# Channel statistics as raw moments of even and odd pixels, summed on TensorE in place of being aggregated on VectorE

## The reference, cut to what matters

```python
def group_norm(x, groups):
    xr = x.reshape(B, groups, -1)
    return ((xr - xr.mean(-1)) * rsqrt(xr.var(-1) + 1e-5)).reshape(x.shape)
x = group_norm(hidden_state, 32)                  # gn1: groups of 2 channels
x = silu(conv2d(x, w0, b0))
x = group_norm(x, 16)                             # gn2: groups of 4 channels
x = silu(conv2d(x, w1, b1, padding=1, groups=4))
x = group_norm(x, 2)                              # gn3, with window gating behind it (gna)
...                                               # gating, 1x1 product with `weight`
x = group_norm(v, 32) + hidden_state              # gn4: groups of 2 channels
...                                               # causal attention over the images, then the experts
```

## Time and profile before

| | before |
|---|---|
| median of 3 runs | 162.06 us (161.11 to 162.81) |
| the profiled execution | 162.24 us |
| its span, first to last instruction | 160.4 us |
| mean granted TensorE clock | 0.989 |
| DVE busy | 100.5 us (63%), 384 instructions |
| ACT busy | 77.0 us (48%), 131 instructions |
| POOL busy | 31.0 us (19%), 27 instructions |
| DMA | 4.63 MB, most of it before 10 us |

### The profile page before, as it was taken

The page is one execution under the profiler, slowest core; times in us unless marked ns, Lnnn a source line. Parts: engine busy times, 40 slices in busy tenths (PEclk is TensorE's granted clock), DMA queues, the critical chain, the costliest instruction groups (busy, mean ns, idle before and its releaser), DMA issues.

```text
span 160.4 us, 2711 instructions
## 1 busy us (share of the span) xinstructions
PE 138.7 (86%) x1001; PEld 62.1 (39%) x1001; DVE 100.5 (63%) x384; ACT 77.0 (48%) x131; POOL 31.0 (19%) x27
## 2 busy tenths in 40 slices
PE   4299689999499769797996989998899999999991
PEld 1144244464134227454824613465244524322230
DVE  0775686695876775618997571078634497993631
ACT  0005400320780042780612999964898869709600
POOL 7046100202130025604046070000610000000000
PEclk9999999999959999999999999999999999999999
DMA  4980000000000000000000000000000000001132
GB/s 119 413 319 1 0 2 4 0 4 0 0 6 0 0 0 0 0 4 0 2 0 0 2 4 0 0 0 0 4 0 0 0 4 0 0 18 48 39 96 65
DMA packets 3740, 4.63 MB, mean 29 GB/s; under 512 B 208, under 2 KB 3408, under 8 KB 3600
## 3 DMA queue, kind: packets, MB, share of 16 engines
q1 hardware_dynamic: 3584, 4.27, 7.7%
q10 hardware_dynamic: 144, 0.20, 0.6%
HBM read 3.42 MB, written 1.05 MB: 28 GB/s over the span
## 4 chain that ended last, share of the span: by engine, by line
PE 61%; DVE 19%; ACT 10%; issue 3%; DMA 2%; POOL 2%; DVEq 0%; ACTq 0%
PE bank L805 10%; PE bank L954 9%; PE bank L929 8%; PE bank L942 7%; PE bank L770 4%; PE bank L763 3%; DMA xin<-x 2%; PE bank L822 2%; PE bank L847 2%; ACT h L400 2%; PE bank L855 2%; DVE ctxs L671 2%; PE bank L750 2%; ACT x L358 2%; PE bank L841 2%
## 5 line engine op out<-in xcount | busy, mean ns | idle before, releaser
L400 ACT ACTIVATE h<-bank,s_bnb,s_bns 128x512 f32<-128x512 f32 x32 | 23.2, 779 | 7.5 <-PE bank L929 7.4
L770 PE MATMUL bank<-warm 128*128 128x512 bf16 x80 | 21.0, 401 | 1.1 <-ACT y L337 1.1
L929 PE MATMUL bank<-xs,par 64*64 64x512 f32 x128 | 17.3, 611 | 1.4 <-ACT h L400 1.4
L805 PE MATMUL bank<-pad,w 32*64 32x512 f32 x288 | 17.0, 593 | 0.4 <-DVE pad L504 0.4
L942 PE MATMUL bank<-h,f2s 64*64 64x512 f32 x128 | 17.0, 602 | 0.2
L337 ACT ACTIVATE y<-bank,par 128x512 f32<-128x512 f32 x8 | 4.8, 688 | 21.0 <-PE bank L805 21.0
L763 PE MATMUL bank<-warm 128*128 128x512 bf16 x32 | 10.9, 487 | 1.3 <-POOL warm L304 1.3
L770 PEld LDWEIGHTS bank<-warm 128*128 128x128 bf16 x80 | 7.8, 106 | 9.9 <-issue 3.1
L805 PEld LDWEIGHTS bank<-pad,w 32*64 32x64 f32 x288 | 7.3, 130 | 7.4 <-issue 5.9
L547 DVE BATCH_NORM_STATS2 s_ws<-y 128x6 f32<-128x64 f32 x64 | 8.8, 209 | 0.3 <-ACT y L337 0.2
L329 ACT ACT_TABLE_LOAD x1 | 1.3, 1283 | 13.9 <-PE bank L776 13.9
(11 more groups left out here) (253 smaller groups left out, 251.3 us busy)
## 6 DMA issues: line engine op xcount, KB each, us to landing
par<-params SPq DMA_DIRECT2D x1, 1516.0 KB, 8.8
xin<-x SPq DMA_DIRECT2D x4, 256.0 KB, 4.3
out<-act SPq DMA_DIRECT2D x4, 256.0 KB, 2.2
row_par<-row_params SPq DMA_DIRECT2D x2, 160.0 KB, 8.7
w<-conv_w SPq DMA_DIRECT2D x1, 288.0 KB, 5.0
par<-params ACTq DMA_DIRECT2D x1, 193.5 KB, 3.8
```

The costliest lines, as they stand in the source:

```text
L400: A.activation(h1[(2 * m + h) % 4][:], bank[Z1[h]][:], ACT.Relu, bias=tile("bnb", P, 3 * EP)[:, col:col + 1], scale=tile("bns", P, 3 * EP) ...
L770: T.matmul(bank[Z1[0]][:], warm[:, 0:P], warm[:], start=True, stop=True)
L805: ins = T.matmul(bank[CONV1[k][2 * j + h]][at:at + C, :], w1[rows, tap, :], pad[rows, b:b + 2, dy:dy + S, dx:dx + S], start=(tap == 0), st ...
L929: ins = T.matmul(bank[Z1[h]][to, :], f1[own, e, to], xs[own, k, q], start=True, stop=True)
```

## The change

After `bn_stats`, DVE no longer aggregates. It squares the eight means (even and odd, four pairs) and scales them by 128, the number of pixels in a half, in one instruction (L481 of the changed kernel), and raises a new semaphore, `moments_ready`, with the last `bn_stats`. PE multiplies the group's matrix with the raw numbers: once with mean and sum of squared deviations of the even pixels (8 columns), once with those of the odd ones, added in PSUM; after `stats_ready` it adds the two sets of squares (4 columns each) onto the second half of the columns. The matrices are divided by the number of pixels, and `group_finish` and `group_shift` multiply the mean by 128 again (`unit`).

```diff
+HALF_PIX = PIX // 2
...
-            def group_finish(name, n, rows=P):
+            def group_finish(name, n, rows=P, unit=1.0):
                 t, _, _ = var_tiles[name]
                 ms, sq = tile(t + "ms", rows, 2, n), tile(t + "sq", rows, n)
                 dve.wait_ge(small_ready, SMALL_AT[name])
                 V.tensor_copy(ms, bank[SMALL][0:rows, 0:2 * n].rearrange("p (a n) -> p a n", a=2)).then_inc(small_free, 1)
                 dve.wait_ge(small_free, SMALL_AT[name])
-                step(V.tensor_tensor(sq, ms[:, 0, :], ms[:, 0, :], ALU.mult))
+                step(V.scalar_tensor_tensor(sq, ms[:, 0, :], unit * unit, ms[:, 0, :], ALU.mult, ALU.mult))
                 V.scalar_tensor_tensor(tile(t, rows, n), ms[:, 1, :], EPS, sq, ALU.add, ALU.subtract).then_inc(var_ready, 1)
-            def group_shift(name, n, rows=P, signal=None):
+            def group_shift(name, n, rows=P, signal=None, unit=1.0):
                 t, _, _ = var_tiles[name]
                 dve.wait_ge(rstd_ready, VAR_AT[name])
-                ins = V.scalar_tensor_tensor(tile(t + "nb", rows, n), tile(t + "ms", rows, 2, n)[:, 0, :], -1.0, rstd(name),
-                                             ALU.mult, ALU.mult)
+                ins = V.scalar_tensor_tensor(tile(t + "nb", rows, n), tile(t + "ms", rows, 2, n)[:, 0, :], -unit, rstd(name), ALU.mult, ALU.mult)
                 if signal is None:
                     step(ins)
                 else:
...
             def channel_stats(name, source, n, arrived=None):
                 t, _, _ = var_tiles[name]
-                raw, mv, e2 = tile(t + "raw", P, n, 6), tile(t + "mv", P, n, 2), tile(t + "e2", P, 2, n)
+                raw, sq = tile(t + "raw", P, n, 6), tile(t + "rsq", P, n, 2)
                 for i in range(n):
                     if arrived is not None:
                         arrived(i)
                     ins = V.bn_stats(raw[:, i, :], source(i))
-                step(ins)
-                for i in range(n):
-                    ins = V.bn_aggr(mv[:, i, :], raw[:, i, :])
-                step(ins)
-                V.tensor_copy(e2[:, 0, :], mv[:, :, 0])
-                step(V.tensor_tensor(e2[:, 1, :], mv[:, :, 0], mv[:, :, 0], ALU.mult))
-                V.tensor_tensor(e2[:, 1, :], e2[:, 1, :], mv[:, :, 1], ALU.add).then_inc(stats_ready, 1)
+                ins.then_inc(moments_ready, 1)
+                dve.wait_ge(moments_ready, MOMENTS_AT[name])
+                means = raw.rearrange("p n (a t) -> p n a t", a=2)[:, :, :, 1]
+                V.scalar_tensor_tensor(sq, means, float(HALF_PIX), means, ALU.mult, ALU.mult).then_inc(stats_ready, 1)
...
+            def moments_product(name, matrix):
+                n = PK
+                t = var_tiles[name][0]
+                raw = tile(t + "raw", P, n, 6).rearrange("p n (a t) -> p a t n", a=2)
+                sq = tile(t + "rsq", P, n, 2).rearrange("p n a -> p a n")
+                small(name)
+                pe.wait_ge(moments_ready, MOMENTS_AT[name])
+                for a in range(2):
+                    T.matmul(bank[SMALL][:, 0:2 * n].rearrange("p (t n) -> p t n", t=2), matrix, raw[:, a, 1:3, :], start=(a == 0), stop=False)
+                pe.wait_ge(stats_ready, STATS_AT[name])
+                for a in range(2):
+                    ins = T.matmul(bank[SMALL][:, n:2 * n], matrix, sq[:, a, :], start=False, stop=(a == 1))
+                ins.then_inc(small_ready, 1)
...
-                "warm": warm_up, "heat": keep_warm, "gn1": lambda k: group_product(("gn1", k), w("gn1"), tile(f"gn1v{k}e2", P, 2 * PK), P, 2 * PK),
-                "xnorm": conv0, "gn2": lambda k: group_product(("gn2", k), w("gn2"), tile(f"gn2v{k}e2", P, 2 * PK), P, 2 * PK),
+                "warm": warm_up, "heat": keep_warm, "gn1": lambda k: moments_product(("gn1", k), w("gn1")),
+                "xnorm": conv0, "gn2": lambda k: moments_product(("gn2", k), w("gn2")),
-                "outp": out_product, "gn4": lambda k: group_product(("gn4", k), w("gn1"), tile(f"gn4v{k}e2", P, 2 * PK), P, 2 * PK),
+                "outp": out_product, "gn4": lambda k: moments_product(("gn4", k), w("gn1")),
...
-    put("gn1", (rows[:, None] // 2 == rows[None, :] // 2) / f(2))
-    put("gn2", (rows[:, None] // 4 == rows[None, :] // 4) / f(4))
+    put("gn1", (rows[:, None] // 2 == rows[None, :] // 2) / f(2 * PIX))
+    put("gn2", (rows[:, None] // 4 == rows[None, :] // 4) / f(4 * PIX))
```

More of the change, by code:

```diff
@@ L187, in conv_attention_experts @@
         stats_ready = sem("stats_ready")
+        moments_ready = sem("moments_ready")
         pads_zeroed, consts_ready, warm_ready = sem_list("pads_zeroed", "consts_ready", "warm_ready")
@@ L234, in conv_attention_experts @@
         SMALL_AT = positions({"gn1", "gn2", "s2row", "gn3", "w2", "gna", "w3", "gn4", "score", "logits", "wt", "wb"})
+        MOMENTS_AT = positions({"gn1", "gn2", "gn4"})
         STATS_AT = positions({"gn1", "gn2", "gn3", "w2", "gna", "w3", "gn4"})
@@ L489, in normalise_x @@
             def normalise_x(k):
-                r, nb = group_shift(("gn1", k), PK)
+                r, nb = group_shift(("gn1", k), PK, unit=HALF_PIX)
                 for i in range(PK):
@@ L499, in normalise_0 @@
             def normalise_0(k):
-                r, nb = group_shift(("gn2", k), PK)
+                r, nb = group_shift(("gn2", k), PK, unit=HALF_PIX)
                 dve.wait_ge(pads_zeroed, k + 1)
@@ L615, in residual1 @@
             def residual1(k):
-                group_shift(("gn4", k), PK, signal=gn4_shift_ready)
+                group_shift(("gn4", k), PK, signal=gn4_shift_ready, unit=HALF_PIX)
                 for i in range(PK):
@@ L720, in _ @@
             stages = {
-                "gn1": gn1_stats, "gn1f": lambda k: group_finish(("gn1", k), PK), "xnorm": normalise_x,
-                "gn2": gn2_stats, "gn2f": lambda k: group_finish(("gn2", k), PK), "norm0": normalise_0,
+                "gn1": gn1_stats, "gn1f": lambda k: group_finish(("gn1", k), PK, unit=HALF_PIX), "xnorm": normalise_x,
+                "gn2": gn2_stats, "gn2f": lambda k: group_finish(("gn2", k), PK, unit=HALF_PIX), "norm0": normalise_0,
                 "bn": lambda k: batch_norm_variances(), "bnf": lambda k: fold_weights(),
@@ L726, in _ @@
                 "w2": window_half, "gna": window_norm_stats, "gnaf": lambda k: group_finish(("gna", k), BK, C),
-                "wan": window_normalise, "gate": gate_y, "gn4": gn4_stats, "gn4f": lambda k: group_finish(("gn4", k), PK),
+                "wan": window_normalise, "gate": gate_y, "gn4": gn4_stats, "gn4f": lambda k: group_finish(("gn4", k), PK, unit=HALF_PIX),
                 "x1": residual1, "ln1": lambda n: layer_norm_stats("ln1", n), "hn": lambda k: layer_norm_scale("ln1", k, hn_ready),
```

## The result

The changed kernel takes 164.12 us (median of 4 runs, 162.50 to 164.84) against 162.38 for the kernel before on the same chip: a ratio of 1.0125, 95% interval 1.0078 to 1.0171. Six more runs of the same kernel beside other runs of before gave 1.0124 (1.0069 to 1.0179). All ratios are taken over the runs within 1.5% of the fastest of their kernel. The change makes the kernel slower by about 2 us. The profiled execution took 164.33 us with a span of 162.5, 2.09 us more than that of before.

The account below looks back on a forecast made before the run. No engine was taken to bound the kernel throughout; up to conv0 PE's queue decides, elsewhere DVE's latency where PE waits. Terms 0.37 + 1.26 - 0.22 + 0.66 - 0.20 - 0.22 = +1.65 us gave 163.7, range 162.6 to 165.0.

Parts of the forecast that it names:

- Eight records for each product, the load of each as its price, whatever the columns: All six products: 2 records become 8; six more cost 1.26 us in the first stage, 0.66 later.
- the 0.66 forecast: At ("gn2", 1), inside PE's conv1 stream: six more records cost +0.66 us and delay the whole of conv1.
- The start 0.88 us earlier where PE waits, -0.20 to -0.22 a place: ("gn2", 0), ("gn4", 0), ("gn4", 1): product starts 0.86 to 0.88 us earlier, records cost 0.66; net -0.22, -0.20, -0.22.
- ("gn1", 0) +0.37, ("gn1", 1) +1.26: First stage: an earlier start of 0.89 us against 1.26 for records at the first product; no gain and +1.26 at the second.
- The first stage is the whole loss, the rest cancels: Three small gains, -0.22, -0.20 and -0.22, pay for +0.66 at ("gn2", 1); the first stage's +0.37 and +1.26 are left.
- Both ways to conv0 lead back to the end of the second product, and neither has slack: Before conv0: DVE's copy and `xnorm`, and PE's warm-up matmuls, both follow the second gn1 product and end nearly together.
- The clock in conv0: conv0's first records: clock level least known; unchanged pace keeps the sum, a clock risen by 13.7 us gives back 0.74.
- The rival that the clock comes at the same time as before: At conv0: clock rises at its old time, so +1.65 - 0.74 = +0.91, 163.0 us; chance 0.2.
- the forecast's own allowance of +0.25: At conv0: +0.25 us on the sum if not even its second record gets a share of the faster clock.
- The stretch at the lower clock behind the windows: Between 44 and 46 us: rival that a 2 us shift spares it, -0.7, giving 163.0, or lengthens it; chance 0.08.
- the forecast's half-chances on either side of 1%: Whole kernel: forecast on the edge of 160.4 to 163.7, its chance halved; slower 0.43, same 0.52, faster 0.05.

Follow-up runs that it names:

- the pair taken out: Changed kernel without one pair of warm-up matmuls between the second gn1 product and conv0: ratio 1.0053, on a repeat 1.008; median of the first eight runs 163.74 us.
- the mixed one: Against the kernel before: two-matmul form at (gn1, 0), (gn2, 0), (gn4, 0), (gn4, 1), DVE aggregation at (gn1, 1), (gn2, 1); ratio 0.9853, 159.2 us.
- the two-matmul form everywhere: Raw moments in two matmuls of 16 and 8 columns instead of the changed kernel's four, at all six products; ratio to the kernel before 0.988, 159.5 us.
- the one with gn1 as before: Changed kernel with gn1 aggregated on DVE as before, gn2 and gn4 in the four-matmul form; ratio to the kernel before 1.001.
- a third with the same queue up to there: Four-matmul form only at (gn2, 0), (gn4, 0) and (gn4, 1), the other three aggregated on DVE; ratio to the kernel before 0.9975.

## Why the prediction was right

It forecast 163.7 us, 162.6 to 165.0, and the mechanism, the place and the size of the loss were those of the runs. That the forecast came so near to 164.12 is in part luck: the sum takes the clock of one execution of before, in which it rose in conv0; of two others with the same queue ahead of conv0 one did the same (1.60 us for its first matmul), and the other had it earlier (1.14); and the median of before moved by 0.32 us, from 162.06 to 162.38, with one more run. Point by point:

- *Eight records for each product, the load of each as its price, whatever the columns.* Right. Six more records took 1.29 us at the lower clock with nothing else changed, where 1.26 was forecast, and the loads of the kernel before follow the columns of weights. At ("gn2", 1) conv1 moved from +1.56 to +2.22, the 0.66 forecast. Sixteen columns in a record cost no more than eight.
- *The start 0.88 us earlier where PE waits, -0.20 to -0.22 a place.* Right. The three copies moved by -0.21 (from +1.77, where `bn_stats` stood, to +1.56), -0.21 and, by ACT's copy behind it, -0.21. Squares caused no second wait.
- *("gn1", 0) +0.37, ("gn1", 1) +1.26.* Right: +0.32 (of it -0.06 by the images) and +1.26, and conv0 at 13.69 where 13.72 stood.
- *The first stage is the whole loss, the rest cancels.* Right within the intervals: 1.0117 with gn1 alone, 1.001 (0.9973 to 1.0047) with all but gn1.
- *"Both ways to conv0 lead back to the end of the second product, and neither has slack".* Right for the changed kernel, by the pair taken out. Incomplete for the kernel before: a third way, over POOL, ended 0.11 us ahead of them. It mattered to no term of the sum.
- *The clock in conv0.* The rival that the clock comes at the same time as before is out, in both profiles: conv0's first matmul took 1.74 and 1.86 us, not 0.86 plus its latency. From conv0's start to the end of ACT's wait the first profile lost 0.16 us of the forecast's own allowance of +0.25; in the second, from conv0 to `bn_stats`, it is 0.29 (3.94 us in place of 3.65), a little over it. Executions of the changed kernel with an early clock are not excluded by this, since only two were profiled.
- *The stretch at the lower clock behind the windows.* It was neither spared nor the same. It came with the shift of the stage, and the windows of the changed kernel (us; busy and records of PE, PEld, DVE, ACT, POOL; granted clock, DMA) answer to the earlier trace rows:

```profile
44.00:46.00 2.00, 0.38 (x4) 0.42 (x6) 1.96 (x15) 2.00 (x5) 0.00 (x0) 1.00 0.00 0
46.00:48.00 2.00, 1.98 (x5) 0.54 (x4) 1.90 (x15) 2.00 (x5) 0.00 (x0) 0.52 0.00 0
48.00:50.00 2.00, 2.00 (x8) 0.92 (x8) 1.38 (x12) 1.77 (x4) 0.66 (x1) 0.62 0.00 0
```

It took 0.27 us more before the ("gna", 0) product than in the kernel before (+2.23 to +2.50). This and the 0.16 in conv0 are what the sum lacked: +1.65 forecast, 1.65 + 0.27 + 0.16 = 2.08, 2.09 measured between the two profiled executions. Both are the clock, both differ from one execution to the next (the profiles of five of the kernels above, the mixed one among them, have no such stretch there, and two of the five have one later, the two-matmul form everywhere at 72 to 76 us with a granted clock of 0.50 and 0.75), and so the forecast's half-chances on either side of 1% were about as good as could be said. The result fell on the slower side.

## What to carry to other kernels

Moving small arithmetic from an engine with latency to PE is priced in records, each an f32 load of 128 columns of weights, 0.11 us at the higher clock and 0.21 at the lower, and not in the columns of the product; so put operands side by side in one matmul and let the instruction that empties PSUM do the addition. Do it where PE sits idle waiting for the result, and leave the longer way on the other engine where PE comes late anyway: the same edit was worth -0.2 us at three places, +0.7 at a fourth and +1.3 at a fifth. Idle waiting alone is no warrant: at ("gn1", 0) PE waits too (4.02 us in the kernel before), but it stands at the lower clock there, and the edit cost 0.3 to 0.4. Ask of every place first which engine is late there, and then at which clock PE works there.

## What the runs showed of the hardware

- The moment at which TensorE's clock rises in the first stage, read from the pace of its records, differs between executions of the same queue. Conv0's first matmul took 1.57 and 1.60 us in the kernel before and in the one with gn1 as before, and 1.14 in a third with the same queue up to there; it took 1.74 and 1.86 in two executions of the changed kernel. The second gn1 product, eight records behind one and the same queue, took 0.65 + 0.85 us in both of those and 0.65 + 0.49 and 0.39 + 0.46 in two executions of the kernel without the pair behind it: there the clock rose at about 11 us, and in the changed kernel at about 15.3 and 16.3. Whether thin records delay the rise isn't shown; these last two have the same thin records.
- A kernel with fewer warm-up matmuls ahead of conv0 had times in two groups, 162.4 to 162.7 and 164.1 to 165.7.
- Taking 0.85 us of warm-up matmuls out of PE's queue gave no gain that could be told from none in two kernels (1.0016, and 0.9838 beside 0.9853), while adding 1.3 us of thin records cost all of it: the way over POOL stands right behind PE's in both kernels, at 0.11 and 0.35 us.
- The first images landed between 4.49 and 5.13 us after the span's start in these profiles, which shifts everything behind by as much.
- The loads of thin f32 records stood 0.11 us apart with 128 columns of weights and 0.06 with 64, at the higher clock.
- A reduction from PSUM over pairs, 16 columns to 8, took 0.17 us on DVE, like the plain copy of 8.
